# Identity products on TensorE ahead of the fifth slot's scores and of the maxima's transposition in the second attention

## What is computed

```python
scores = jnp.einsum('bqhd,bkhd->bhqk', qd, kd) * D ** (-0.5)
scores = jnp.where(mask, scores, -jnp.inf)
lse = jax.nn.logsumexp(scores, axis=-1)
o = jnp.einsum('bhqk,bkhd->bqhd', jnp.exp(scores - lse[..., None]), vd)
...
w = jnp.exp(lse_all - m)
w = w / w.sum(0)
out = sum((o * wi.astype(o.dtype) for o, wi in zip(outs, w)))
return out.transpose(0, 2, 1, 3).reshape(B, L, E) @ Wo.T + bo
```

## Time and profile before

| | |
|---|---|
| time before, median of 3 runs | 839.02 us (836.04 to 843.04) |
| the profiled execution's own time | 833.27 us |
| its span, first to last instruction | 831.6 us |
| TensorE busy in the span | 636.9 us (77%) |
| VectorE busy in the span | 507.0 us (61%) |
| ScalarE busy in the span | 421.5 us (51%) |
| GpSimd busy in the span | 342.0 us (41%) |
| mean granted TensorE clock | 0.862 |

### The profile page before, as it was taken

The page is one execution under the profiler, slowest core; times in us unless marked ns, Lnnn a source line. Parts: engine busy times, 40 slices in busy tenths (PEclk is TensorE's granted clock), DMA queues, the critical chain, the costliest instruction groups (busy, mean ns, idle before and its releaser), DMA issues. The chain is left out here.

```text
span 831.6 us, 14880 instructions
## 1 busy us (share of the span) xinstructions
PE 636.9 (77%) x4859; PEld 475.3 (57%) x4859; DVE 507.0 (61%) x1757; ACT 421.5 (51%) x826; POOL 342.0 (41%) x472
## 2 busy tenths in 40 slices
PE   6998899699999999999234879777888630148995
PEld 5777787477877877777112446554555420036773
DVE  1565757766566567555026577778765619867752
ACT  2535433476577567656111557555655511037772
POOL 2423322576525734832212445344533312034754
PEclk9989999799999999999655789888987955569997
DMA  5452223546536435531311122213300014025653
GB/s 165 148 173 83 77 89 107 157 138 168 137 83 145 105 90 135 115 72 18 52 44 47 60 65 76 78 57 90 91 29 28 26 39 152 0 60 147 157 110 39
DMA packets 73873, 75.95 MB, mean 91 GB/s; under 512 B 8037, under 2 KB 66449, under 8 KB 73553
## 3 DMA queue, kind: packets, MB, share of 16 engines
q1 hardware_dynamic: 61217, 59.32, 23.1%
q0 software_dynamic: 10928, 15.57, 10.9%
q10 hardware_dynamic: 1664, 0.27, 0.2%
HBM read 52.20 MB, written 22.94 MB: 90 GB/s over the span
## 5 line engine op out<-in xcount | busy, mean ns | idle before, releaser
L2001 DVE CUSTOM_DVE_ANT_0 c_sn<-c_ps_s,k_mask 128x128 f32<-128x128 f32 (+1 forms) x256 | 75.7, 351 | 55.7 <-PE c_ps_s L2139 55.5
L1525 PE MATMUL b_ps_y<-b_w2h,b_hh 128*128 128x256 f16 x320 | 87.3, 273 | 4.5 <-DVE e_xl L1418 4.2
L1335 POOL DMA_INDIRECT res<-b_y,b_s_idx x40 | 72.8, 1820 | 42.3 <-ACT b_y L1377 30.7
L1833 POOL TENSOR_SCALAR_AFFINE_SELECT c_pr<-c_pr 128x512 f32<-128x512 f32 x64 | 42.8, 670 | 110.3 <-ACT c_pr L1892 109.3
L1525 PE MATMUL b_ps_y<-b_w2l,b_hh 128*128 128x256 f16 x320 | 87.2, 273 | 0.0
L1525 PE MATMUL b_ps_y<-b_w2h,b_hl 128*128 128x256 f16 x320 | 87.2, 273 | 0.0
L1409 DVE TENSOR_TENSOR b_hl<-b_h,b_hh 128x640 f16<-128x640 f32 x64 | 52.8, 825 | 40.6 <-ACT b_hh L1357 40.4
L1321 POOL DMA_INDIRECT e_xg<-rows,e_g_idx x35 | 39.7, 1135 | 75.2 <-DVE e_g_idx L1436 62.1
L2167 PE MATMUL c_ps_v<-c_pr,k_vx 128*64 128x256 f32 (+1 forms) x512 | 66.2, 387 | 5.2 <-POOL c_pr L1833 4.9
L1892 ACT ACTIVATE c_pr<-c_ps_t 128x768 f32<-128x768 f32 x64 | 51.7, 807 | 15.6 <-PE c_ps_t L2153 15.6
L1490 PE MATMUL b_ps_h<-e_xh,e_w1h 128*128 128x320 f16 x256 | 57.0, 305 | 2.9 <-PEq L135 2.1
(11 more groups left out here) (427 smaller groups left out, 1754.8 us busy)
## 6 DMA issues: line engine op xcount, KB each, us to landing
e_w<-in_L_ffn_W_dram SPq DMA_DIRECT2D x16, 1024.0 KB, 5.3
d_w<-in_L_ffn_W_down_dram SPq DMA_DIRECT2D x8, 640.0 KB
k_ks<-kT SPq DMA_DIRECT2D x48, 64.0 KB, 2.6
c_qs<-q SPq DMA_DIRECT2D x48, 64.0 KB, 2.3
d_w<-in_L_ffn_W_up_dram SPq DMA_DIRECT2D x4, 682.0 KB, 5.3
rows<-a_rows SPq DMA_DIRECT2D x8, 264.0 KB, 2.7
rows<-c_rows SPq DMA_DIRECT2D x8, 264.0 KB, 2.2
a_x_in<-in_x_dram SPq DMA_DIRECT2D x8, 256.0 KB, 3.9
```

Of the source, the lines that this page charges most:

```text
L1335: pool.indirect_dma_start(out=dram["res"], out_offset=bass.IndirectOffsetOnAxis(ap=s_idx[u][:, j:j + 1], axis=0), in_=y[:, j, :], in_offse ...
L1525: last = pe.matmul(ps_y[(j + CT) % 2][:, 0:D], a, b[:, f, :], start=(f == 0 and k == 0), stop=(f == FC - 1 and k == 2))
L1833: pool.affine_select(out=late, in_=late, compare_op=ALU.is_ge, fill=0.0, base=0, pattern=[[0, 2], [0, 2], [1, P]], channel_multiplier=-1). ...
L2001: dve.tensor_tensor_reduce(sn[r][:, a:b], ps_s[:, r, a:b], mask[:, a:b], -1.0, 3.0e38, ALU.add, ALU.min, mx[g % 2][:, q, r, j:j + 1]).then ...
```

## The change

A new helper `hold_clock(bank, times)` multiplies the f16 identity by itself, read four times side by side (512 columns), into a whole PSUM bank, `times` times. Nothing reads the result. In slot 4 of steps 0 to 7 it is called twice with `ps_a`: eight products ahead of the scores of f, and four behind these scores, ahead of the transposition of the maxima. Three waits stand in front of the first call, for the copies out of `ps_a`. In steps 6 and 7 there are no scores of f, and in step 7 no transposition; there all twelve products stand together.

```diff
+            def hold_clock(bank, times):
+                for _ in range(times):
+                    pe.matmul(bank[:].rearrange("p (a b) -> p a b", b=P), ident_h[:],
+                              ident_h[:].unsqueeze(1).to_broadcast([P, 4, P]), start=True, stop=True)
+
             over_tensor(pe)
...
                     if p < 4 and within(g):
                         scores(g, p + 4)
+                    if p == 4 and within(n):
+                        after(pe, s_xT, min(f, B - 1))
+                        after(pe, s_x3T, l)
+                        after(pe, s_oT, l)
+                        hold_clock(ps_a, 8)
                     if p >= 4 and within(f):
                         scores(f, p - 4)
+                    if p == 4 and within(n):
+                        hold_clock(ps_a, 4)
                     if p == 4 and within(g):
                         after(pe, s_mlo, g)
                         done(pe, s_av, n * HH + p)
```

## The result

The median fell from 838.65 us (831.88 to 845.55) to 835.88 us (827.35 to 847.04), 20 runs each. The ratio is 0.9944 with a 95% interval from 0.9919 to 0.9969, that is 4.7 us faster, with bounds of 2.6 and 6.8. It takes the fast runs alone, which leaves out 6 of the 20 after and 3 of the 20 before; the medians of all runs lie 2.8 us apart and their means 3.4, so the sign stands and the size is about 3 to 5 us. The forecast was 841.1 us, 2.1 slower. The result lies in the range of 831 to 850, and it is within 1% as the likeliest case said, but its sign is the other one.

A forecast was written before the change was run, and what follows sets the result against it. It took a step as a ring of waits, with ScalarE's and GpSimd's chain binding behind the transposition. Terms -2.0 + 0.5 - 0.2 + 0.2 + 1.0 + 2.6 = +2.1 us on 839.02 gave 841.1 us, range 831 to 850.

The forecast's parts named there:

- the likeliest case: Whole kernel: a time within 1% of the one before, chance 0.73.
- The delay in step 0: Step 0's transposition comes 1.2 us later behind the products; less a gain of 0.68, +0.5 us.
- in step 7: Last step: no wait to fill, so twelve products at full clock delay everything behind; +2.6 us.
- the 2.5 us that I had for TensorE itself: Steps 2, 3 and 5: TensorE's work up to the projection shrinks by 2.5 us at full clock, the step by less.
- Steps 2, 3 and 5 ... I take 0.68: Products fit the gaps; the first `weighted` ends 0.68 us sooner, and so does ScalarE's run; three steps, -2.0 us.
- the same 0.68 in step 1: Step 1: the transposition is delayed by 0.5 us, less a gain of 0.68; -0.2 us.
- rival A: Ring runs through TensorE: steps 0 to 6 each gain 2.5 us; -9.6 us, 829.4 us; chance 0.17.
- 1.0 hidden in step 6: Step 6: of ScalarE's 2.0 us delay about 1 us is hidden by TensorE's slow work; +1.0 us.
- the delays of steps 4 and 6: The transposition moves by 0.9 us in step 4 and 2.7 in step 6, with products partly at half clock.
- B: Identity products do not hold the clock, which falls where it does now; +14.4 us, 853.4 us; chance 0.12.
- C: The clock falls behind the new wait for `xn`, costing 2.5 us in half of steps 1 to 5; 847.3 us; chance 0.15.

The follow-up runs named there:

- experiment 3: The changed kernel with five more products ahead of the turn of `xn` in steps 0 to 4; 834.68 us, ratio to before 0.9965.
- experiment 5: The changed kernel with GpSimd making the scale of `xn` ahead of the gate values; 831.72 us, ratio to before 0.9964.
- experiment 2: The changed kernel with its products in steps 3 and 5 alone; one profiled run, 843.95 us.
- experiment 11: The changed kernel with five more products in slot 6 of step 5; one profiled run, 834.21 us.
- experiment 8: The changed kernel without products in steps 0 and 7, two ahead of `xn` in steps 1 to 4, scale first, gate exponentials later; 825.72 us, ratio to before 0.9878.
- experiment 4: The changed kernel with twice as many f32 transposes of the identity in place of the products; 836.26 us, ratio to before 0.998.
- experiment 1: The changed kernel without the products of step 7, but with twelve in step -1; 833.18 us, ratio to before 0.9919.
- experiment 10: The changed kernel with batch l's gate exponentials on ScalarE moved from slot 4 to slot 5; one profiled run, 832.74 us.
- experiment 12: The changed kernel without the four products ahead of the transposition, the eight kept; one profiled run, 835.27 us.
- experiment 7: The changed kernel without step 7's products, twelve in step -1, five more ahead of `xn` in steps 1 to 4; 833.54 us, ratio to before 0.9972.
- experiment 9: As experiment 8, with six products in step 0's gap and four ahead of its turn of `xn`; 827.55 us, ratio to before 0.9899.

## Why the prediction was right and wrong

**Right.** The placement of the twelve in every step, and the 0.215 us for one where I estimated 0.218. The delay in step 0 (1.36 for 1.2; 1.0 in the mean over the profiles) and in step 7 (2.70 for 2.6). The clock held over the gaps, with stretches of 3.40 us in steps 1 and 6 as assumed for step 1. In step 2, `mrow` came sooner, ScalarE ran without idle to the exponentials, TensorE reached the projection of `o` 3.18 us after its first `weighted` and not 5.61, which is the 2.5 us that I had for TensorE itself, and it waited 1.12 us for `xn` where 1.2 was forecast. The step gained 0.61 us for 0.68.

**Wrong: "Steps 2, 3 and 5 ... I take 0.68", for step 5, and with it the same 0.68 in step 1.** I had read ScalarE's run without idle in step 2 and taken it as the bound of every step. That run is made of the gate exponentials of batch l and ends in the `xn` of batch e, and both exist only in steps 2 to 4. There the gain was 0.61 to 1.15 us, and experiments 3 and 5 show that the chain over ScalarE and GpSimd binds. In step 1 there is no batch l, in steps 5 and 6 no batch e. There gains near rival A's size came: 1.83 us in step 1 beside its delay, 2.41 in step 5 (1.28 and the delay of 1.13 at its end), 1.73 in step 6 (2.70 - 0.97). Experiment 2 shows the gain of step 5 without the delay (2.20), and experiments 3 and 11 show that work added on TensorE lengthens step 1 and step 5, though only by 0.4 and 0.5 of itself. Why slow work taken away there was worth 1.8 to 2.4 us of the 2.5 that TensorE gained, and work added only half of itself at most, stays open. For step 1 experiment 8 fits as well: with the scale ahead of the gate values and the exponentials out of the way, which is what the missing batch l means there, the steps 2 to 4 too take 24.92 us, and step 1 takes 24.97. For step 6 it is only argued. Step 0, with neither l nor m, has no projection of `o` behind its transposition, and gained 0.58.

The sum of the gains was 9.15 us for the 5.8 that I had (seven times 0.68, and 1.0 hidden in step 6). That is 3.4 of the 5.7 us between +2.1 and -3.6. Step 5 brings 1.73 of it and step 1 1.15, the middle steps 2 to 4 another 0.56 (2.60 for 2.04). In step 6 the gain came out as I had it in all, 1.73 for 0.68 and 1.0, though I had put the larger part down to hiding.

**Wrong by size: the delays of steps 4 and 6.** I had the delay in step 4 at 0.9 us and in step 6 at 2.7, from falls taken where one execution had shown them, at 573.92 and 625.12. In the profile after no fall stood ahead of the gap of step 4, and the delay was 0. In step 6 the stretch was 3.40 us, not 6.8, and the delay 1.13. Together with step 1 (0.34 for 0.5) the delays were 5.5 for 7.9: the other 2.4 us.

**The rivals.** A came near in steps 1, 5 and 6 (1.7 to 2.4 us of its 2.5) and is refuted in the others. The measured -3.6 us lies halfway between its -9.6 and my +2.1. B fell with the first look at 522.72 (1.00), and its reason with experiment 4. C's mechanism was seen: falls behind the wait for `xn` in one middle step each of experiments 1, 2, 4 and 11, and in step 0 of 5, 10 and 12. Its price is 1.4 to 1.7 us in the middle steps (27.85 or 27.89 for 26.23 to 26.45) and 1.1 to 1.8 in step 0 (26.20 to 26.89 for 25.14), not 2.5, and no profile has it in more than one of these steps.

**Open.** Why the clock falls behind that wait in one middle step of an execution and not in the others. None of the four kernels that fill it (3, 7, 8 and 9) had a fall in steps 2 to 4. But of the eight profiles with products that do not fill it, four had no fall behind it there either (after, 5, 10 and 12), so this can be chance, and the timed runs of 7 against 1 show no gain.

## What to carry to other kernels

Products that hold the clock over a gap are worth only what the chain behind the gap owes to TensorE. Work that out for each kind of step, those that fill and drain the pipeline too, because a batch that is not there takes the binding chain away with it. Put such products only where there is a wait to fill: in the last step they cost their full 2.7 us. And look for the wait that the faster engine now has further on: there the clock can fall next, in a denser place, and the engines that it waits for (here GpSimd's order, 0.75 us a step) are the next thing to shorten. When a condition is moved from one batch to another (here from n to g), look at both ends of the pipeline: it takes the work out of one step and can put it into another.

## What the runs showed of the chip

Before, the clock fell at gaps of one or two waits, of 1.0 to 2.2 us each; in the later kernels it also fell behind single waits of 1.1 to 1.4 us, in steps in which TensorE is busy for 21 to 24 of 27 us. What a stretch at 1.2 GHz cost depended on where it lay: under the first `weighted` and the projection of `o` 0.6 to 1.2 us a step, under the projection of `xn` 1.1 to 1.8, behind the gap of steps 1, 5 and 6 1.7 to 2.4; the short one at 528.8 in experiment 12 nothing. Its length was 3.40 us in steps 1 and 6 after, with the products in it, and 6.8 or 10.2 before, but 6.8 also in step 6 of experiments 4, 8, 11 and 12; what decides it stays open. And transposes held the clock as products did, at 1.00 from 538.6 to 620 us of experiment 4.
